# A zeroed warm-up for TensorE, an early table load, and a maximum with zero moved behind transposes, in a one-core network of convolution, attention and expert layers

## The reference

```python
x = _L0_conv_ref(x, ...)      # non-local block: theta, phi, g (1x1), 2x2 max pool, softmax,
                              # wz, batch norm over the batch's own statistics, + x
x = _L1_conv_ref(x, ...)      # below
t = _to_tokens(x)             # 8 x 256 tokens x 256
t = t + _L2_attn_ref(_ln_t(t), ...)
t = t + _L2_ffn_ref(_ln_t(t), L2_ffn_weight)
t = t + _L3_attn_ref(_ln_t(t), ...)
t = t + _L3_ffn_ref(_ln_t(t), ...)
x = _from_tokens(t, x)
```

```python
residual = x
h = _shift_conv(x, w1)
h = _shift_conv(h, peg_w, stride=1, pad=1, groups=64, bias=peg_b)
h = jax.nn.relu(_bn(h, bn1_g, bn1_b, bn1_m, bn1_v))
h = _shift_conv(h, w2, stride=1, pad=1)
h = jax.nn.relu(_bn(h, bn2_g, bn2_b, bn2_m, bn2_v))
h = _shift_conv(h, w3)
h = _bn(h, bn3_g, bn3_b, bn3_m, bn3_v)
return jax.nn.relu(h + residual)
```

## Time and profile before

| | |
|---|---|
| median of 3 runs | 665.81 us |
| lowest, highest | 664.83, 666.66 us |
| the profiled execution's own time | 665.75 us |
| its span (first to last instruction) | 664.0 us |
| mean granted TensorE clock over the span | 0.964 |
| PE busy | 593.3 us, 89% |
| DVE busy | 447.8 us, 67% |
| ACT busy | 326.7 us, 49% |
| POOL busy | 117.8 us, 18% |

### The profile page before, as it was taken

One profiled execution on the slowest core, in us unless ns is written; L12 is line 12 of the kernel. 1 busy time (PEld: TensorE's weight loads), 2 busy tenths in 40 slices (PEclk: granted clock), 3 DMA queues, 4 the chain that ended last, 5 costly groups with the idle time before them and its releaser, 6 DMA issues.

```text
span 664.0 us, 11227 instructions
## 1 busy us (share of the span) xinstructions
PE 593.3 (89%) x4159; PEld 407.7 (61%) x4206; DVE 447.8 (67%) x1275; ACT 326.7 (49%) x548; POOL 117.8 (18%) x115
## 2 busy tenths in 40 slices
PE   5884776768999999999999979999999999999897
PEld 2653334656767767767767757576675756565443
DVE  4767858758477577677677584776858576676464
ACT  2436658617566566566566554343443535353110
POOL 2031000260313313303303302011030200000000
PEclk9985998789899999999999988999999999999999
DMA  9500000375134134134134141204040230000000
GB/s 335 216 0 0 1 0 6 82 212 168 50 99 146 44 107 146 33 116 139 37 113 138 30 120 55 89 25 135 1 142 18 62 98 17 1 17 0 17 13 19
DMA packets 40253, 50.64 MB, mean 76 GB/s; under 512 B 4052, under 2 KB 33492, under 8 KB 39892
## 3 DMA queue, kind: packets, MB, share of 16 engines
q1 hardware_dynamic: 40200, 49.94, 24.3%
HBM read 35.11 MB, written 14.68 MB: 75 GB/s over the span
## 4 chain that ended last, share of the span: by engine, by line
PE 60%; DVE 15%; issue 3%; ACT 2%; DMA 1%; SPq 1%; POOL 0%; DVEq 0%; ACTq 0%
PE ps L1252 14%; PE ps L1135 8%; PE ps L1127 7%; PE ps L1209 5%; PE ps L1198 5%; DVE nmax L1419 4%; PE ps L1119 4%; PE ps L1194 3%; PE ps L1178 3%; PE ps L1170 3%; PE ps L1216 2%; DVE acc L1499 2%; PE ps L1173 2%; DVE xn L1375 2%; DVE stats L1364 2%
## 5 line engine op out<-in xcount | busy, mean ns | idle before, releaser
L1419 DVE TENSOR_REDUCE nmax<-ps 128x2 f32<-128x512 f32 (+1 forms) x192 | 130.7, 687 | 79.5 <-PE ps L1178 52.1
L1312 ACT ACTIVATE PT<-ps 128x512 f32<-128x512 f32 x192 | 113.3, 598 | 115.7 <-PE ps L1198 114.0
L1252 PE MATMUL ps<-wm,xnT 128*128 128x512 f32 x256 | 119.9, 599 | 0.7
L1079 POOL TENSOR_TENSOR rstd<-ve,fix 128x2 f32<-128x2 f32 x32 | 22.2, 695 | 321.6 <-DVE ve L1370 321.6
L1306 ACT ACTIVATE QS<-ps 8x1024 bf16<-8x1024 f32 x64 | 65.1, 1017 | 27.3 <-PE ps L1183 25.3
L1198 PE MATMUL ps<-QS,KS 110*128 110x256 bf16 (+3 forms) x512 | 74.7, 247 | 0.0
L1499 DVE SCALAR_TENSOR_TENSOR acc<-ps,gate,acc 128x256 f32<-128x256 f32 x128 | 61.6, 481 | 18.5 <-PE ps L1252 16.2
L1252 PEld LDWEIGHTS ps<-wm,xnT 128*128 128x128 f32 x256 | 45.1, 190 | 39.7 <-issue 38.1
L1127 PE MATMUL ps<-xnT,by_dim 128*128 128x256 f32 x256 | 63.4, 394 | 2.2 <-ACT xnT L1277 2.2
L1099 POOL TENSOR_TENSOR parts<-rest,fix 128x512 bf16<-128x512 f32 x30 | 38.1, 1270 | 139.8 <-DVE rest L1388 100.5
L1194 PE MATMUL ps<-fixb 128*128 128x256 bf16 (+1 forms) x192 | 60.0, 312 | 2.3 <-DVE nmax L1419 2.0
(11 more groups left out here) (211 smaller groups left out, 925.9 us busy)
## 6 DMA issues: line engine op xcount, KB each, us to landing
parts_dram<-parts SPq DMA_DIRECT2D x32, 384.0 KB, 3.0
QS<-parts_dram SPq DMA_DIRECT2D x96, 128.0 KB
KS<-parts_dram SPq DMA_DIRECT2D x96, 128.0 KB, 2.6
wt<-wt_dram SPq DMA_DIRECT2D x1, 2562.0 KB, 19.5
wm<-wm_dram SPq DMA_DIRECT2D x1, 2449.0 KB, 14.0
xc<-x_dram SPq DMA_DIRECT2D x8, 256.0 KB, 5.7
out_dram<-res SPq DMA_DIRECT2D x8, 256.0 KB, 2.1
w<-w_dram SPq DMA_DIRECT2D x1, 845.0 KB, 8.8
```

The costliest lines, as they stand in the source:

```text
L1252: mm = pe.matmul(d, normT(stage, batch)[:, c, t * P:(t + 1) * P], M("We", c * EXPERTS * CH + e * 2 * CH, 2 * CH), start=(c == 0), stop=(c ...
L1312: act.activation(PT[:, pt_slot(piece, n), :], bank(piece), ACT.Exp).then_inc(drain(piece), 1)
L1419: dve.tensor_reduce(group[:, 0, :] if part == 0 else group[:, 1, 2 * part - 2:2 * part], bank(piece).rearrange("p (j n) -> p j n", n=w_), ...
```

## The change

It has three edits.

1. DVE zeroes a tile `warm`, which is the first 512 columns of `dwq` (the depthwise weights, written for good much later, at L766 of before). PE then makes 18 products (`WARM_UPS`) of 128x512 bf16 of this tile with itself into PSUM bank 7, ahead of its wait for `w0` and x. Nobody reads the result. Bank 7 is written again by the scores.
2. ACT calculates the exponential of one column of the zeroed tile into `sc_inv` (written for good later), ahead of its wait for `w0`.
3. `x2` and its eight ACT instructions (L701) go. The bias is instead added by ACT in place to `x1`: three of the eight pieces behind L695 in the round k = 1, three in the round k = 2, the last two ahead of the end part. DVE's L922 now waits for the piece with its bias. PE turns `pre` itself as soon as DVE has written a quarter's two halves. The maximum with zero is taken as the banks leave PSUM: ACT takes out banks 0 to 6 with it, DVE bank 7.

```diff
+WARM_UPS = 18
...
-            x2 = z
...
+            warm_ready = sem("warm_ready")
+            warm = dwq[:].rearrange("p a n -> p (a n)")[:, 0:512]
...
-            x2_ready = sem("x2_ready")
+            x1_biased = sem("x1_biased")
...
+                pe.wait_ge(warm_ready, 1)
+                for _ in range(WARM_UPS):
+                    pe.matmul(ps[:, 7, :], warm[:, 0:P], warm, start=True, stop=True)
                 pe.wait_ge(w0_loaded, 16)
...
                 for n in range(8):
-                    pe.wait_ge(x2_ready, 2 * (n // 2) + 2)
+                    pe.wait_ge(res_added, 2 * (n // 2) + 2)
...
-                                              x2[:, c, t * P:(t + 1) * P], F("ident"))
+                                              pre[:, c, t * P:(t + 1) * P], F("ident"))
...
+                act.wait_ge(warm_ready, 1)
+                act.activation(sc_inv[:, 0:1], warm[:, 0:1], ACT.Exp)
                 act.wait_ge(w0_loaded, 16)
...
+                def add_bias(n):
+
+                    x_ = x1[:, n % NC2, n // NC2 * QUART:(n // NC2 + 1) * QUART]
+                    act.activation(x_, x_, ACT.Identity, bias=bnb[2][:, n % NC2:n % NC2 + 1]).then_inc(x1_biased, 1)
...
+                        add_bias(6)
+                        add_bias(7)
...
-                for q in range(4):
-                    sl = slice(q * QUART, (q + 1) * QUART)
-                    for o in range(NC2):
-                        act.wait_ge(res_added, 2 * q + o + 1)
-                        act.activation(x2[:, o, sl], pre[:, o, sl], ACT.Relu, bias=bnb[2][:, o:o + 1]).then_inc(x2_ready, 1)
-                for n in range(0, 8, 2):
+                        for n in range(3 * k - 3, 3 * k):
+                            add_bias(n)
+                for n in range(7):
                     act.wait_ge(tok_done, n + 1)
                     act.activation(X[:, 2 * n:2 * n + 2, :].rearrange("p a n -> p (a n)"), ps[:, (4 + n) % 8, :],
-                                   ACT.Copy).then_inc(tok_out_act, 1)
+                                   ACT.Relu).then_inc(tok_out_act, 1)
...
+                dve.memset(warm, 0.0).then_inc(warm_ready, 1)
                 for q in range(4):
...
                         dve.wait_ge(conv_done, 12 + n + 1)
+                        dve.wait_ge(x1_biased, n + 1)
                         dve.scalar_tensor_tensor(pre[:, o, sl], ps[:, (4 + n) % 8, :], aff_a[2][:, o:o + 1], x1[:, o, sl],
                                                  ALU.mult, ALU.add).then_inc(res_added, 1)
-                for n in range(1, 8, 2):
-                    dve.wait_ge(tok_done, n + 1)
-                    dve.tensor_copy(X[:, 2 * n:2 * n + 2, :].rearrange("p a n -> p (a n)"), ps[:, (4 + n) % 8, :])\
-                       .then_inc(tok_out_dve, 1)
+                dve.wait_ge(tok_done, 8)
+                dve.tensor_scalar(X[:, 14:16, :].rearrange("p a n -> p (a n)"), ps[:, 3, :], 0.0, None, ALU.max)\
+                   .then_inc(tok_out_dve, 1)
```

## The result

| | before | after |
|---|---|---|
| median of 10 runs | 664.91 us | 660.89 us |
| lowest, highest | 664.30, 666.66 us | 659.31, 663.78 us |
| profiled execution's own time | 665.75 us | 662.70 us |
| its span | 664.0 us | 660.9 us |
| mean granted clock | 0.964 | 0.966 |

The ratio is 0.9939 with a 95% interval from 0.9925 to 0.9953: 4.0 us faster, between 3.1 and 5.0. That is more than the 2.7 us forecast, and 660.89 lies under the range's lower end of 661.5. The ten runs of before have a median 0.9 us under that of the three runs shown ahead of the prediction. The profiled execution of after, at 662.70 us, is one of its slower ones: it won 3.05 us.

What follows compares the result with a forecast made beforehand. It took PE, busy for 593.3 us of a 664.0 us span, as the bound. 665.75 less 2.0 (start) and 0.7 (end) gave 663.05, with 0.06 for the runs' median 663.1 us; range 661.5 to 665.3 us.

Steps and rivals of the forecast that it cites:

- The start's term: First block's start: 18 products end at 7.95 us, theta at 14.83 in place of 16.86; gain 2.0 us.
- The end's term: First block's end: PE's transposes start at 107.8 us, end at 113.1 in place of 113.77; gain 0.6 to 0.9, taken 0.7.
- The sum: Whole kernel: 665.75 - 2.0 - 0.7 = 663.05, with 0.06 us for the median of the runs 663.1 us.
- I let every microsecond won ahead of 114.8 us count in full: First block: time won before the second block's first ACT instruction reaches the kernel's end undiminished.
- The table load: ACT's 1.28 us load at 11.06 us moves into the wait for x; costed and credited at nothing.
- The bias additions: Eight on ACT, six in gaps of 2.21 and 2.20 us, leaving 0.1 us in each; costed at nothing.
- `wm`: Needed by the first expert transposes: landed at 21.04 us, wanted at 22.0; holds until the gain is 3.0 us.
- The slower rivals: At the start: zeroes don't wake the clock, 667.3 us, chance 0.06; the memset waits for POOL, 667.2 us, chance 0.02.
- zeroes wake the clock: Against the rival at the start that zero products stay at 1.2 GHz, theta ending at 19.0 us: 667.3 us, chance 0.06.
- the memset: Rival at the start: DVE's memset held until POOL's zeroing ends at 5.19 us, theta ending at 19.0: 667.2 us, chance 0.02.
- the gain was not lost behind another wait: Against the rival that another wait takes up PE's gain at the start, only the end counting: 665.1 us, chance 0.05.
- the early rise: Rival: clock rises early at the start, theta gains 2.6 us, the end 0.9: 662.3 us, or 661.8; chance 0.13.

Runs made afterwards that it cites:

- products alone: Only the memset and the 18 products on PE added to the kernel before: 663.33 us, ratio 0.9973 (0.9962 to 0.9983).
- the end alone: Only the third edit (bias additions moved, maximum behind the transposes, x2 gone) on the kernel before: 663.73 us, ratio 0.9979 (0.9967 to 0.9990).

## Why the prediction was wrong

Its direction and its mechanisms held; its sizes and its range did not. The step that failed is that it read the slow stretches of TensorE's clock off one profile and carried them over unchanged, at the start ("I take 5.4 us, since it is the row at the same place"), at the end ("4 fast until 108.2, 15 slow until 111.6"), and with no width for those behind them.

*The start's term.* The clock rose 4.7 us after the first product in the profile of after, and between 2.9 and 5.9 us after it over the eleven profiles with 18 products. The products took 0.43 and 0.21 us and not 0.46 and 0.23. So theta started at 7.37 us in place of the forecast 7.95, and phi gained 2.63 us in place of 2.0. But the 5.4 us was itself one case of several: with the queue of before phi also started at 14.97 and 15.28 us. Over the profiles, the mean start of phi is 15.93 us in the four that start as before does and 14.29 in the eleven with 18 products, 1.6 us earlier; the start of the first layer's last product is 37.9 to 38.6 us in those four and 34.2, 36.0 and 37.3 us with the whole change, 2.5 us earlier in the mean. The products alone measured 1.8 us (1.1 to 2.5) in the median. So the forecast's 2.0 is not refuted as a number; it came near because phi's start was taken too late on both sides, 16.86 us for a mean of 15.93 and 14.83 for a mean of 14.29, and that is luck.

*The end's term was mis-sized.* The forecast took a slow stretch at 108.2 us over from before, and got 0.7 us. In the profile of after the clock was not low there at all, and DVE's sums, not PE, were last: 0.89 us. Where the clock was low, the old end took 9.92 us and the new one 7.87. By itself the edit was worth 1.4 us (0.7 to 2.2).

*The baseline.* The sum started from 665.8; ten runs of before have 664.9. Of the 2.2 us between forecast and result, 0.9 lie in this starting point and 1.3 in the gain (4.0 in place of 2.7). Of these 1.3 the end alone has 0.7 (1.4 in place of 0.7), the products alone have none (1.8 in place of 2.0), and the rest is what the parts do not add up to. The second block, which no edit touches, took 549.2 us in both profiles of before and 548.0, 547.8 and 549.2 in those of the whole change. Whether that is chance stays open.

*The range.* It was built on "runs 1.8 us apart" for before, and on terms that are fixed once the clock's rise is known. But a shift of the program also moves where the clock is low later, in the first block and in the second, and the ten runs of after lie 4.5 us apart. A term for that, on both sides, was put at nothing, by "I let every microsecond won ahead of 114.8 us count in full". The profiled execution of after, at 662.70 us, lies within the range; the median does not.

*What held.* In the median each microsecond at the start reached the end nearly in full (36 products: 3.9 us in, 3.5 us out, with a width of 2.1 to 5.1); in single executions it did not. The table load is worth nothing that could be measured. The bias additions fit into ACT's gaps, with 0.36 us to spare where 0.1 was forecast, at a pace of 0.61 us and not 0.66. `wm` was not waited for. The slower rivals did not happen: zeroes wake the clock; the memset ran from 0.86 us for 0.27 us beside POOL's memset of 2.26 us, so the two did not hold each other up; and the gain was not lost behind another wait.

*The rival that came nearest* is the early rise, which had a chance of 0.13: theta gains 2.6 us and the end 0.9, as the profile of after shows (2.63 and 0.89), though the clock rose after 4.7 us and not after 3.1. Its 662.3 us is 0.4 under that execution's 662.70. Started from the 664.9 of the ten runs it would have given 661.4, and the median was 660.89.

*The two rules of the Trainium skill.* That transposes don't count as busy for the clock ("TensorE: Matmul & The Clock Gate", "Part 4: PE-mode transpose") is not borne out here: in the profile of after the clock stays at 2.4 GHz through 32 transposes that leave PE idle for 0.22 us between pairs, and the end is 0.89 us shorter. Where it was low at that place it rose while PE did transposes alone, 3.05 us after the first one in before, and only 6.1 us after it in the run with the products alone (first transpose at 105.68 us, granted clock 0.50 up to 111 and 0.60 from 111 to 112 us). That one kernel's number of slow products differs from run to run (same page, "Part 1: The HAM clock gate") does agree, and it was the more important: of the same 18 products between 7 and 14 were slow, and phi's start lay between 13.6 and 14.9 us.

## What to carry to other kernels

Where TensorE waits for its first data, products of a zeroed tile up to that moment are worth having (1.8 us here). Count them so that they reach it: eight, which did not, worked in one profile and not in another, and thirty-six cost about what they ran over. Moving an elementwise step from between two engines to a copy that must be made anyway is worth more than its own length where the engine behind it may be slow. And where the clock falls behind idle stretches, read the forecast of a shift from several profiles of the kernel before, and give it the width of the runs of both kernels, not that of one.

## What the runs showed of the hardware

- Products of zeroes raise TensorE's clock as those of data do: with the first one at 1.19 us, the pace of the products doubled at 5.9 us in the profile of after, and between about 4.1 and 7.1 us over the eleven profiles with 18 of them.
- TensorE's clock rose during transposes alone: at 111.6 us in before (transposes from 108.59 us) and at about 111.8 us in the run with the products alone (transposes from 105.68 us).
- The first quarter of x was there between 6.0 and 7.1 us (start of DVE's first pooling) in the eighteen profiles, with the same transfers ahead of it; this moves theta where nothing else holds it.
- The granted clock reads 1.00 before its first change in an execution although passes are at half speed (0.85 us in theta before, 0.43 us for 512 bf16 columns); the distance between weight loads tells the truth there.
- After the clock had risen, an idle time of 1.84 us left it high for theta in one execution, and one of 2.39 us was followed by half clock in another.
- Where the clock was low without them, 45 products of zeroes in idle stretches nearly halved the time of the softmax's products (2.00 us in place of 3.66). They shortened the first block by 1.2 us in one pair of executions, 0.2 us in another, and the medians by nothing that could be told apart.
- The same second block took from 544.3 to 549.4 us. Its length goes with the granted clock in two stretches (130 to 180 and 380 to 410 us), most plainly in the lowest two; what decides where it falls from one execution to the next was not tried, and stays open.
